# Row sums of a graph layer turned by VectorE in 32x32 blocks, stored in four pieces

## The reference, cut to what matters

```python
h = jnp.maximum(_layernorm(x, axis=-1), 0.0)
A_fwd  = [A1, A2, shifted]                       # A1 = A2 = adj
A_list = A_fwd + [jnp.swapaxes(a, 1, 2) for a in A_fwd] + [eye]
HW  = einsum('bnf,rfo->rbno', h, W[:, :F]) + einsum('rd,rdo->ro', W_edges, W[:, F:])[:, None, None, :]
AHW = einsum('rbnm,rbmo->rbno', A, HW)
x   = x + jnp.max(AHW, axis=0) + b
```

## Time and profile before

| what | us |
|---|---|
| median of 3 runs | 221.49 (220.02 to 223.38) |
| the profiled execution, its own time | 222.73 |
| its span, first to last instruction | 220.9 |
| around the span (222.73 less 220.9) | 1.8 |

### The profile page before, as it was taken

The page is one execution under the profiler, slowest core; times in us unless marked ns, Lnnn a source line. Parts: engine busy times, 40 slices in busy tenths (PEclk is TensorE's granted clock), DMA queues, the critical chain, the costliest instruction groups (busy, mean ns, idle before and its releaser), DMA issues.

```text
span 220.9 us, 4961 instructions
## 1 busy us (share of the span) xinstructions
PE 205.4 (93%) x1009; PEld 166.4 (75%) x1009; DVE 190.4 (86%) x403; ACT 186.8 (85%) x468; POOL 170.1 (77%) x179
## 2 busy tenths in 40 slices
PE   7879949889999999999999999999999999999980
PEld 5567727678887888887888888888888878888860
DVE  4698549869898998999898998999899989979783
ACT  3779739599999999999999999999999999999540
POOL 1470685966979797997979797988979797979441
PEclk9999996999999999999999999999999999999996
DMA  4978969679789898889898898879898898563626
GB/s 150 344 122 190 245 149 208 157 144 282 144 250 201 223 223 198 251 152 269 151 292 162 261 193 239 202 168 250 151 301 159 263 188 234 125 143 50 155 36 95
DMA packets 122384, 42.64 MB, mean 193 GB/s; under 512 B 102807, under 2 KB 112135, under 8 KB 122375
## 3 DMA queue, kind: packets, MB, share of 16 engines
q1 hardware_dynamic: 121287, 42.41, 79.9%
q10 hardware_dynamic: 1088, 0.13, 0.4%
HBM read 38.27 MB, written 4.26 MB: 192 GB/s over the span
## 4 chain that ended last, share of the span: by engine, by line
PE 76%; DMA 8%; DVE 5%; SPq 4%; ACT 3%; issue 2%; DVEq 0%; ACTq 0%
PE rel_ps L821 10%; PE rel_ps L823 10%; PE rel_ps L822 10%; PE at_ps L795 8%; PE bwd_ps L821 6%; PE bwd_ps L823 6%; PE bwd_ps L822 6%; PE fwd_ps L821 6%; PE fwd_ps L823 6%; PE fwd_ps L822 6%; SPq L210 3%; DMA x_sb<-in_x 3%; PE turn_ps L806 3%; DMA a_sb<-in_adj 2%; DMA sum_all<-sums_dram 2%
## 5 line engine op out<-in xcount | busy, mean ns | idle before, releaser
L334 POOL TENSOR_TENSOR a_lo<-a_sb,a_hi 128x512 fp32r<-128x512 f32 x62 | 81.1, 1330 | 29.1 <-ACT a_hi L417 29.1
L468 ACT ACTIVATE rel_ps<-sum_all,c_col 128x512 f32<-128x512 f32 (+1 forms) x63 | 41.6, 673 | 8.8 <-DVE best L639 6.6
L639 DVE TENSOR_TENSOR best<-rel_ps,best 128x512 f32<-128x512 f32 x62 | 42.4, 684 | 4.5 <-PE rel_ps L823 3.3
L417 ACT ACTIVATE a_hi<-a_sb 128x512 fp32r<-128x512 f32 x64 | 39.6, 633 | 4.0 <-DMA a_sb<-in_adj 4.0
L610 DVE TENSOR_TENSOR at_lo<-at_ps,at_hi 128x512 fp32r<-128x512 f32 x47 | 32.1, 686 | 3.9 <-ACT at_hi L428 3.0
L428 ACT ACTIVATE at_hi<-at_ps 128x512 fp32r<-128x512 f32 x47 | 27.7, 590 | 3.5 <-PE at_ps L795 3.4
L821 PE MATMUL fwd_ps<-at_hi,h_hi 128*128 128x512 f32 x64 | 26.7, 417 | 1.0 <-DVE at_lo L610 1.0
L821 PE MATMUL bwd_ps<-a_hi,h_hi 128*128 128x512 f32 x64 | 26.8, 419 | 0.3 <-POOL a_lo L334 0.3
L349 POOL TENSOR_TENSOR xb_sb<-xp_sb,bias_sb 128x512 f32<-128x512 f32 x16 | 22.8, 1422 | 5.3 <-DMA xp_sb<-in_x 5.3
L823 PE MATMUL bwd_ps<-a_hi,h_lo 128*128 128x512 f32 x64 | 25.4, 398 | 0.0
L822 PE MATMUL bwd_ps<-a_lo,h_hi 128*128 128x512 f32 x64 | 25.3, 395 | 0.0
(11 more groups left out here) (107 smaller groups left out, 475.3 us busy)
## 6 DMA issues: line engine op xcount, KB each, us to landing
a_sb<-in_adj SPq DMA_DIRECT2D x28, 512.0 KB, 4.1
sum_all<-sums_dram SPq DMA_DIRECT2D x16, 512.0 KB, 5.9
x_sb<-in_x SPq DMA_DIRECT2D x16, 256.0 KB, 5.0
xp_sb<-in_x SPq DMA_DIRECT2D x64, 64.0 KB, 2.9
a_blocks<-in_adj SPq DMA_DIRECT2D x60, 64.0 KB, 2.3
out<-o_sb SPq DMA_DIRECT2D x60, 64.0 KB, 5.0
a_sb<-in_adj SPq DMA_DIRECT2D x8, 256.0 KB, 5.8
w_sb<-in_L_gnn_W SPq DMA_DIRECT2D x1, 448.0 KB, 5.9
```

What stands on the lines that cost most here:

```text
L334: pool.tensor_tensor(a_lo[q][:, j, :], a_sb[q][:, j, :], a_hi[q][:, j, :].bitcast(fp32), ALU.subtract).then_inc(a_lo_ready[j], 1)
L417: act.activation(a_hi[q][:, j, :], a_sb[q][:, j, :], ACT.Copy, accum_out=sums[q][:, 0, j:j + 1]).then_inc(a_hi_ready[j], 1)
L468: act.activation(to[:, cols], sum_all[q][:, 0 if r in FWD else 1, cols], ACT.Copy, scale=c_col[:, r:r + 1]).then_inc(after_it, 1)
L639: dve.tensor_tensor(best[q][:], held[:], best[q][:], ALU.max).then_inc(joined[r], 1)
```

## The change

`sums` becomes a zeroed tile of 128x32 whose first eight columns are used. VectorE turns it as four 32x32 blocks into `sum_rows`, also 128x32, where partition 32g + s holds sum column s of the nodes of group g. TensorE's turn and ScalarE's copy go, with the waits that guarded their PSUM bank. VectorE's turn stands behind `split_at` of block 3 in each step, in front of `split_bwd` (in batch 1 behind `round_h`; in batch 0 between the last `split_at` and `split_ht`). SyncE stores four pieces of 8x32 in place of one of 8x128.

```diff
-        sums = pair(sb, "sums", [P, 2, C])
-        sum_rows = pair(sb, "sum_rows", [S, P])
+        sums = pair(sb, "sums", [P, Q])
+        sum_rows = pair(sb, "sum_rows", [P, Q])
...
                 sp.wait_ge(sum_rows_ready, 2 * k + q + 1)
-                sp.dma_start(sums_dram[q][:, :], sum_rows[q][:]).then_inc(sums_stored[q], 16)
+                for g in range(G):
+                    sp.dma_start(sums_dram[q][:, g * Q:(g + 1) * Q],
+                                 sum_rows[q][g * Q:g * Q + S, :]).then_inc(sums_stored[q], 16)
...
-                sp.wait_ge(sums_stored[q], 16 * (k + 1))
+                sp.wait_ge(sums_stored[q], G * 16 * (k + 1))
...
+            for q in range(2):
+                pool.memset(sums[q][:], 0.0)
             pool.memset(minus_one[:], -1.0).then_inc(consts_ready, 1)
...
-                wait(act, sums_turned, b - 1)
+                wait(act, sum_rows_ready, b - 1)
...
-            def take_sums(k, q, turned_ps=turn_ps):
-                act.wait_ge(sums_turned, 2 * k + q + 1)
-                wait(act, sums_stored[q], 16 * k)
-                act.activation(sum_rows[q][:], turned_ps[0:S, 0:P], ACT.Copy).then_inc(sum_rows_ready, 1)
...
+            def turn_sums(k, q):
+
+                b = 2 * k + q
+                dve.wait_ge(a_hi_ready[C - 1], b + 1)
+                dve.wait_ge(at_hi_ready[C - 1], b + 1)
+                wait(dve, sums_stored[q], G * 16 * k)
+                dve.transpose(sum_rows[q][:], sums[q][:]).then_inc(sum_rows_ready, 1)
...
                     split_at(k, q, 3)
+                    turn_sums(k, q)
                 split_bwd(*prev)
...
-                if not any(is_batch(b, n) for n in range(3)):
-                    pe.wait_ge(sum_rows_ready, b)
...
-                pe.transpose(to[0:S, 0:P], sums[q][:].rearrange("p t c -> p (t c)"), ident[:]).then_inc(sums_turned, 1)
...
-                    if is_batch(b, 0) or is_batch(b, 1):
-                        pe.wait_ge(sum_rows_ready, b + 1)
```

More of the change, by code:

```diff
@@ L148, in gnn_layer @@
         at_lo_ready = [sem(f"at_lo_ready{i}") for i in range(C)]
-        sums_turned, sum_rows_ready = sem("sums_turned"), sem("sum_rows_ready")
+        sum_rows_ready = sem("sum_rows_ready")
         xb_ready = sem("xb_ready")
@@ L415, in round_a @@
                 wait(act, bwd_done, b - 1)
-                wait(act, sums_turned, b - 1)
+                wait(act, sum_rows_ready, b - 1)
                 act.activation(a_hi[q][:, j, :], a_sb[q][:, j, :], ACT.Copy,
-                               accum_out=sums[q][:, 0, j:j + 1]).then_inc(a_hi_ready[j], 1)
+                               accum_out=sums[q][:, j:j + 1]).then_inc(a_hi_ready[j], 1)
             def round_at(k, q, i):
@@ L426, in round_at @@
                 wait(act, fwd_done, b - 1)
-                wait(act, sums_turned, b - 1)
+                wait(act, sum_rows_ready, b - 1)
                 act.activation(at_hi[q][:, i, :], at_from(b, i)[:], ACT.Copy,
-                               accum_out=sums[q][:, 1, i:i + 1]).then_inc(at_hi_ready[i], 1)
+                               accum_out=sums[q][:, C + i:C + i + 1]).then_inc(at_hi_ready[i], 1)
             def normalise(k, q):
@@ L482, in first_step @@
                 act.activation(w_hi[:], w_sb[:], ACT.Copy).then_inc(w_hi_ready, 1)
-                take_sums(0, 0, rel_ps[1])
                 round_at(*ahead, 0)
@@ L503, in step @@
                 join_first(k, q)
-                if not second:
-                    take_sums(k, q)
                 if second:
@@ L524, in step @@
                     round_at(*ahead, 0)
-                    if second:
-                        take_sums(k, q, rel_ps[1])
                 else:
@@ L689, in step @@
                     round_h(*ahead)
+                if is_batch(b, 1):
+                    turn_sums(k, q)
                 join(*prev, FWD[1])
@@ L754, in _ @@
                 split_at(0, 0, i)
+            turn_sums(0, 0)
             split_ht(0, 0)
@@ L898, in first_step @@
                 bwd(0, 0, 3)
-                turn_sums(0, 0, rel_ps[1])
                 turn_a(*ahead, 0)
@@ L923, in step @@
                 fwd(k, q, 1)
-                if not is_batch(b, 1):
-                    turn_sums(k, q)
                 eye(k, q, EYE[1])
@@ L934, in step @@
                     turn_h(*ahead)
-                if is_batch(b, 1):
-                    pe.wait_ge(joined[EYE[1]], b + 1)
-                    turn_sums(k, q, rel_ps[1])
                 bwd(k, q, 0)
```

## The result

| what | before | after |
|---|---|---|
| median, us | 221.18 (6 runs, 220.02 to 223.38) | 236.57 (6 runs, 233.16 to 238.97) |
| ratio to before, 95% interval | | 1.0597 (1.053 to 1.0665) |
| the profiled execution, its own time / its span | 222.73 / 220.9 | 235.84 / 234.0 |

The change makes the kernel slower by 6%. The ratio leaves out three of the six executions after, which took 237.3 to 239.0 us where the other three took 233.2 to 235.8, so it says 0.0597 x 221.18 = 13.2 us and not the 15.4 between the two medians. The forecast of 238.5 us was 1.9 above the median, but that nearness is in part chance: the two profiled executions lie 235.84 - 222.73 = 13.1 us apart, where the forecast had 17.1.

The account below looks back on a forecast made before the run. TensorE bounds the loop at 12.27 us a step, with SyncE's queue a second loop of 12.21 that the stores make the bound. Delay of 16.6 plus 0.5 at the end, 17.1 us, gave a forecast of 238.5; range 224 to 243.

Parts of the forecast that it names:

- Rival A: SyncE's long reload_x issue shrinks by what is added ahead, TensorE stays the bound; about 221 us, no change; chance 0.15.
- the 1.30: Time in us that three more store issues add to SyncE's queue in each batch, at 0.43 each.
- B: SyncE's round gives half back: a_blocks loads still run, small stores could issue in 0.28; 0.6 us a round, 229; chance 0.12.
- C: TensorE's turn costs its row's full 0.27 us, its waits hide more, SyncE gives time back; 217.2 us; chance 0.05.
- One issue: SyncE's queue: each small store takes 0.384 us in the median plus some 0.05 between issues, so 0.43.
- The twelve rounds: Loop, batches 2 to 13: each of SyncE's twelve rounds becomes 1.30 us longer, 15.6 in total.
- The start: Batches 0 and 1: SyncE's extra issues delay the chain by 1.1 and 1.30 us, together 2.4.
- The slack: Loop's last spread: it landed 1.4 us before ScalarE's fill started, so 1.4 comes off SyncE's delay of 18.0.
- The end: Batches 14 and 15: load_xp and the store behind it stand late in SyncE's order; 0.5 us, between 0 and 1.5.
- The VectorE term: VectorE's new 128x32 turn ahead of split_bwd takes 0.22 us, hidden by 0.23 us of idle time; taken as 0.
- TensorE's: Removing the turn from TensorE's stream saves 0.10 us each, 1.6 us for sixteen, as long as TensorE bounds.
- a delay of SyncE is swallowed between the spread and its landing: SyncE's queue from spread to landing is bound by the DMA engines; reload_x's long issue absorbs any delay there.

Follow-up runs that it names:

- e1: Kernel before plus three extra 8x32 stores that nobody reads, on SyncE's queue behind the store of the sums, in twelve loop steps; 231.79 us, ratio 1.0485.
- e3: Kernel before with its 8x128 tile of sums stored as four 8x32 pieces, turn still on TensorE; 235.08 us, ratio 1.0598.
- e7: Changed kernel with its four stores issued by ScalarE behind the second fill in place of SyncE; 221.12 us, ratio 0.997.
- e9: Kernel before, turn on TensorE and copy on ScalarE, with its one 8x128 store issued by ScalarE in place of SyncE; ratio 0.992.
- e8: Changed kernel with one store of all 128 partitions, issued by ScalarE, in place of SyncE's four; ratio 0.9921.
- e5: Kernel before plus 24 already satisfied semaphore waits on SyncE's queue ahead of reload_x in twelve loop steps, no transfer; 221.92 us, ratio 1.0019.
- e2: Kernel before plus three extra 8x32 stores on SyncE's queue between the output stores and reload_x, in twelve loop steps; 233.19 us, ratio 1.0458.

## Why the prediction was right, and where its sizes were off

What bounds: right. SyncE's queue was a second loop just below TensorE's step, and the change pushed it above. e1, e3 and e7 show it from three sides: issues alone cost most of it, the stores alone cost all of it, the same stores on another queue leave the time of before. In the kernel before the queue did not yet bound the loop (the step is 12.27 there and in e9 alike). Rival A, that the 1.30 would be given back, fell: 1.01 us were added and the round grew by 1.09. The growth of the round lies between B's 0.6 and the forecast's 1.30. Of B's two reasons the first fell, nothing was given back; the second, small stores that issue in 0.28, holds for three of the four. C fell with the time.

The sum, term by term, in the profiled executions:
- One issue: 0.43 predicted, and (1.39 - 0.38) / 3 = 0.34 measured. The first of the four stores takes 0.38, as the single one did, and each of the other three about 0.29; I had used the 0.38 for all. The tile of the changed kernel has it in the median. This term carried the largest part of the error (3.2 of the rounds' 15.6).

```profile
L254 SPq DMA_DIRECT2D sums_dram<-sum_rows x64: 282/295/1276, 14.3 to 217.2; - x64
```

- The twelve rounds: 15.6 predicted. The spreads of batches 1 and 13 are 196.57 - 40.43 = 156.1 apart, and were 183.97 - 40.23 = 143.7: 12.4 measured.
- The start: 2.4 predicted, 0.2 measured (batch 1's spread at 40.43 in place of 40.23). Two reasons can be read. In batch 0 VectorE turns at 13.04, so the stores leave at 14.31, a microsecond before the single one did, and the bias behind them is in time. In batch 1 the spread had waited 1.92 us for the single store to land; now the last of the four is issued at 39.17 and lands 1.24 later. From first store to spread it takes 2.36 us where it took 1.94, so 0.4 more and not 1.30; why the last one landed sooner, the runs don't tell.
- The slack: the loop's last spread leaves 12.6 us later than before and takes 0.5 longer to land (6.4 us, 5.9 before), which was not in the sum; less the slack of 1.4 the fill of 191.29 comes 11.8 us later, at 203.09.
- The end: it takes 30.9 us from that fill on, 1.3 more than before, where 0.5 was predicted. In the last step ScalarE's fill at 222.09 stands 2.29 us for the spread, a wait that the kernel before does not have and the prediction did not name.
- Sum: 17.1 predicted, 13.1 measured. The terms were off by 3.2 and 2.2 one way and by 0.5 and 0.8 the other, so that part of the errors cancelled.

The VectorE term (0.22 predicted for the turn, 0.20 measured, and hidden in the loop, as e8's step shows) and TensorE's (0.10 a turn, 0.09 measured in e8 against e9) were right.

What was wrong in the reasoning is the sentence that a delay of SyncE is swallowed between the spread and its landing. e5 and e2 split it: bare time is, a further transfer is not. It made no difference here, because the new stores stand in the other part. For somebody who wanted to mend the kernel by moving the stores up in the queue it would have been a costly error: e2's three transfers cost 4.6%.

The figure of the Trainium skill that was weighed ("DMA: Bandwidth & Descriptors", section "Anatomy of one DMA — SWDGE (gpsimd) path", some 50 ns of dispatch) is given there for GpSimd's path and does not carry over to SyncE's queue here: the cheapest of 64 issues took 282 ns, and three more in a round cost 6% of this kernel. The transpose figures beside rival C are the page's for a tile in bfloat16, not for this float32 turn of 128x8.

## What to carry to other kernels

A queue that waits for nobody and has almost the period of the bounding engine becomes the bound with the next issue that is added: add up a round of issues and compare first. Splitting a 4 KB store in four cost this queue three issues of 0.34 us; try one transfer over all partitions, or another engine's queue with idle time, first. When a change that saves on the bounding engine shows nothing in the total, compare the step within the loop and then look at the last step.

## What the runs showed that I had not expected

The fifth issue behind the spread. In the kernel before and in e2 it ends with the spread's landing or shortly ahead of it, and its transfer is of 256 KB in one and of 1 KB in the other. So the size of the transfer that is held up doesn't matter. Whether the limit is one on the number of transfers ahead, on their rows or on something else, the runs don't tell: the spread and four output stores stood ahead in all of them.

A TensorE that came back at half speed after a wait. In the start of the changed kernel TensorE stood 4.16 us for a fill, and the stretch behind it has a granted clock of 0.51 of full speed, that is near the lower of its two levels, 1.2 GHz; in the kernel before the same wait was 1.56 us and the same stretch has 1.00. The kernel before has such a stretch too, at another place: TensorE stands 2.92 us for a fill until 33.43, and from 33.3 to 36.7 the granted clock is 0.50. The windows of the changed kernel (after the stretch: TensorE, its loads, VectorE, ScalarE and GpSimd busy, with counts, clock, DMA share, GB/s):

```profile
38.00:44.00 6.00, 3.00 (x12) 2.12 (x12) 4.19 (x8) 2.01 (x6) 5.84 (x9) 1.00 0.53 131
44.00:51.00 7.00, 5.84 (x19) 4.87 (x20) 1.74 (x4) 4.31 (x10) 2.48 (x2) 0.51 0.82 144
```

The fill behind it is 14.4 us after the last (44.41 to 58.78), where before it was 12.1. How much of this is the clock and how much the late spread, and whether any of it is left in the total, the rows don't tell apart, and no run tried it.
